# Second stage of a transformer kernel on one core: TensorE's waits ahead of runs of small matmuls, repeated waits dropped, every engine's work in another order

## The chip, the cores and the metric

The kernel runs on one core of a Trainium2 chip. The metric is the device time of the whole program in microseconds (us). The core has five engines with instruction streams of their own, which meet only at semaphores: TensorE (PE; its loads of stationary data are PEld), VectorE (DVE), ScalarE (ACT), GpSimd (POOL), and SyncE (SP), which here issues DMAs.

## The reference

The input has 8 samples of 512 tokens of 128 values, all in 32 bit. A first layer of attention (16 heads of 8, weights by an iteration on 1/(lambda - s)) comes first. Then come six layers of local attention and a gated feed-forward part; this is the second stage, and the change touches it alone:

```python
for i in range(6):
    x = attn_layer(shift_tokens(x), Wqkv[i], q_scale[i], k_scale[i], Wo[i]) + x
    x = ffn_layer(shift_tokens(x), ln_g[i], ln_b[i], W1[i], b1[i], W2[i], b2[i]) + x

def attn_layer(x, Wqkv, qs, ksc, Wo):      # 16 heads of 64
    q, k, v = split(x @ Wqkv)
    q, k = l2norm(q) * qs, l2norm(k) * ksc
    q, k = rotary(q), rotary(k)            # with a scale that grows with the position
    # windows of 32 tokens, each looks at itself and at the one before it
    attn = softmax(mask(8 * q @ k.T))
    return (attn @ v) @ Wo

def ffn_layer(x, g, bln, W1, b1, W2, b2):  # 341 hidden values
    a, gate = split(layernorm(x) * g + bln @ W1 + b1)
    return a * gelu(gate) @ W2 + b2
```

## The kernel before

Stage 1 does the first attention, stage 3 turns the result back and adds it. Stage 2 runs 48 steps: a step `n` is one sample through one layer (6 layers of 8 samples). The work of a step is cut in pieces, and each engine runs the pieces in an order that is written out in a function `body(b)` of its own. A body mixes pieces of step `b`, of `b - 1` and of `b - 2`, so that three steps are under way at once; `live(b, back)` leaves out those that do not exist. On TensorE and the other compute engines the first four bodies are peeled, and then a loop follows. TensorE's loop has a hint for its back edge, and its head stands at slot 0 of an instruction fetch block.

The pieces go by groups of four heads, `g` = 0 to 3:
- `q{g}`, `k{g}` (`project`, L1319): two matmuls of 512 columns each into two PSUM banks. ScalarE squares them (`squares`, L1550), k or q first by its order; VectorE multiplies them by two tables each (`rotate`, L1809 and L1810, which waits for the square); GpSimd adds the squares (`square_sums`, L1698) and the products (`add_rotated`, L1702).
- `norm{g}` (`norms`, L1326) sums the squares; ScalarE makes the inverse norm (L1555, L1564); VectorE finishes (`finish`, L1833), and eight DMAs (`rotated`, L1210) spread the result.
- `score{g}` (`scores`, L1342): 64 matmuls on tiles of 64 by 32, in two parts. VectorE masks and takes the maximum (L1817, L1824), GpSimd subtracts it (L1708), ScalarE takes the exponential (L1580), VectorE sums and inverts (L1839, L1846), GpSimd normalises (L1713).
- `turn{g}` (`turn`, L1354): eight transposes of 128 by 128; ScalarE copies them out (`turned`, L1586).
- `v{i}` (`values`, L1391); ScalarE copies it (L1573); DMAs roll it (`rolled`).
- `weigh{g}` (`weigh`, L1375): 64 matmuls of 32 columns, in two parts; VectorE copies them out (`weighted`, L1853).
- `wo` (L1401), `mean` (L1407), `var` (L1412), `gate0`, `gate1`, `up0`, `up1` (`hidden`, L1416) and `out` (`ffn_out`, L1441) are the output projection and the feed-forward part. VectorE's `residual` (L1864), `centre`, `scale`, `gate` (L1885) and `finished` (L1894), ScalarE's `log_variance`, `inverse_deviation` and `gelu`, and GpSimd's `affine` (L1723) go with them. At each new layer VectorE runs `tables(l)` ahead of its body.

A matmul of 32-bit data leaves two records of TensorE in the trace, and two of the load.

The eight PSUM banks are dealt by hand in a list, `HOLD`, in TensorE's order: the name of a piece, how many steps it lags, and its first bank. Pieces in `ONE` hold one bank, the others two. `take(name, b)` (the wait is L1306) looks back in the list for whoever held the banks last, and waits for the semaphore that says that they are empty (`EMPTIED`):

```python
EMPTIED |= {f"q{g}": [(s_rot[0], NG, g)], f"k{g}": [(s_rot[1], NG, g)],
            f"norm{g}": [(s_lnn, NG, g)], f"score{g}": [(s_mask, NG, g)], f"turn{g}": [(s_pTev, NG, g)],
            f"weigh{g}": [(s_oT, NG, g)], f"v{g}": [(s_vev, NG, g)]}
```

So the banks of a `q` are empty when VectorE has rotated it, and those of `up0` when VectorE has multiplied both gates. A wait on TensorE is an instruction of its own, `pe.wait_ge` followed by `pe.sem_inc(held["pe"], 1)`, and stands right ahead of the matmuls that need it.

Of the kernel before, what the change touches and what calls it, by code (L numbers as in the profile page):

```python
# [989 lines left out]
def stage2(nc, consts, wqkv, wod, w1d, w2d, vecd, hist):  # L990
    with ExitStack() as ctx:
# [116 lines left out]
        def live(b, back):  # L1108
# [31 lines left out]
        def _(sp):  # L1140
# [107 lines left out]
            def body(b, l, k):  # L1248
# [4 lines left out]
                if live(b, 3):  # L1253
                    store(b - 3)
                if live(b, 2):
                    load_w2(b - 2, l, k == 2)
                if live(b, 1):
                    rotated(b - 1, 2)
                if live(b, 0):
                    load_projections(b, l, k == 0, (2, 3))  # L1260
                if live(b, 0):
                    load_xs(b)
                if live(b, 1):
                    rolled(b - 1, 1)
                if live(b, 1):
                    rotated(b - 1, 3)
                if live(b, 0):
                    rotated(b, 0)
                if live(b, 0):
                    rotated(b, 1)  # L1270
                if live(b, 1):
                    load_vectors(b - 1, l, k == 1)
                if live(b, 0):
                    load_xr(b)
                if live(b, 0):
                    rolled(b, 0)
                if live(b, 1):
                    load_w1(b - 1, l, k == 1)
                if live(b, 0):
                    load_wo(b, l, k == 0)  # L1280
# [6 lines left out]
            for b in range(STEPS, STEPS + 3):  # L1287
                body(b, DEPTH, b - STEPS)
# [4 lines left out]
        def _(pe):  # L1293
# [16 lines left out]

            def project(n, g, which, out):
                pe.wait_ge(wg_in[g], 16 * n + 16)
                pe.sem_inc(held["pe"], 1)
                if g == 0:
                    pe.wait_ge(xs_in, 32 * n + 32)
                    pe.sem_inc(held["pe"], 1)
# [5 lines left out]
            def norms(n, g, out):  # L1322
                pe.wait_ge(s_sqs, at(n, g))
                pe.sem_inc(held["pe"], 1)
# [5 lines left out]
            def scores(n, g, part, out):  # L1330
                p = g % 2
                if part == 0:
                    pe.wait_ge(q_in[p], 128 * at(n, g // 2, 2))
                    pe.sem_inc(held["pe"], 1)
# [14 lines left out]
            def turn(n, g, out):  # L1349
                pe.wait_ge(s_pr, at(n, g))  # L1350
                pe.sem_inc(held["pe"], 1)
# [5 lines left out]
            def weigh(n, g, part, out):  # L1357
                if part == 0:
                    pe.wait_ge(s_pTev, at(n, g))
                    pe.sem_inc(held["pe"], 1)  # L1360
                if part == 0 and g % 2 == 0:
                    pe.wait_ge(s_vev, at(n, g + 1))
                    pe.sem_inc(held["pe"], 1)
                    pe.wait_ge(vr_in[g // 2], 48 * n + 96)
                    pe.sem_inc(held["pe"], 1)
# [16 lines left out]
            def values(n, i, out):  # L1382
                half, part = i // 2, i % 2
                if part == 0:
                    pe.wait_ge(wg_in[2 * half], 16 * n + 16)
                    pe.sem_inc(held["pe"], 1)
                    pe.wait_ge(wg_in[2 * half + 1], 16 * n + 16)
                    pe.sem_inc(held["pe"], 1)
# [55 lines left out]
            def body(b):  # L1444
# [24 lines left out]
                if live(b, 2):  # L1469
                    ups(b - 2, 1, take("up1", b))  # L1470
# [679 lines left out]
```

## Time and profile before

| | us |
|---|---|
| median of 3 runs | 4945.61 (4935.18 to 4952.09) |
| the profiled execution's own time | 4938.53 |
| its span, first to last instruction | 4936.4 |
| TensorE busy | 4103.4 (83%) |
| VectorE busy | 4056.8 (82%) |
| GpSimd busy | 3516.9 (71%) |
| ScalarE busy | 2979.7 (60%) |

Busy time of an engine is the time under its instructions; waits, branches and DMA issues do not count. Stage 2 takes up some two thirds of the span, from about 1540 to 4900 us. In the rows below, a bracket in a timeline is the engine's idle time ahead of that row, and what ended it; "issue" means that nothing the profile shows did.

### The profile page before, as it was taken

What the parts mean: (1) busy time and instruction counts of PE and PEld (TensorE: products, weight loads), DVE (VectorE), ACT (ScalarE), POOL (GpSimd) and SP (SyncE); (2) the same over time, 40 slices, a digit from 0 to 9 for tenths busy, and PEclk for the clock granted to TensorE, in tenths of its full rate; (3) what the DMA queues carried; (4) which work ended last, traced back from release to release, by engine and by line L of the source; (5) the groups of instructions that cost most, each with busy time, mean ns of one, the idle gap of its engine ahead of it and who ended that gap; (6) DMA issues with size and microseconds to landing.
All of it is one profiled execution on the core that took longest, in us unless ns stands there. A gap on an engine that the chain in (4) does not pass through costs nothing. (4 is left out here: it accounts for less than half of the span.)

```text
span 4936.4 us, 154683 instructions
## 1 busy us (share of the span) xinstructions
PE 4103.4 (83%) x60260; PEld 2147.1 (43%) x60260; DVE 4056.8 (82%) x7132; ACT 2979.7 (60%) x4240; POOL 3516.9 (71%) x1655
## 2 busy tenths in 40 slices
PE   3666666666647999899999999899998999899995
PEld 1233223233223555455544555455554555455552
DVE  6999999999956888788878888788887888788883
ACT  5999999999953555445544555455544555455441
POOL 4999999999965676666766676567665766576661
PEclk9755555555558999999999999999999999999997
DMA  0000000000004444444553444444444444444443
GB/s 14 3 5 9 5 9 5 5 9 5 7 8 107 114 113 109 113 103 109 116 123 92 107 113 109 99 114 111 109 114 97 113 109 109 98 118 109 108 98 82
DMA packets 234267, 382.36 MB, mean 77 GB/s; under 512 B 38432, under 2 KB 63776, under 8 KB 233504
## 3 DMA queue, kind: packets, MB, share of 16 engines
q1 hardware_dynamic: 229408, 371.06, 31.9%
q8 instruction: 488, 8.00, 0.7%
q10 hardware_dynamic: 4224, 2.10, 0.1%
q14 instruction: 147, 1.20, 0.1%
HBM read 51.89 MB, written 18.87 MB: 14 GB/s over the span
## 5 line engine op out<-in xcount | busy, mean ns | idle before, releaser
L734 POOL TENSOR_TENSOR W<-W 128x1280 f32<-128x1280 f32 x416 | 954.9, 2319 | 141.2 <-ACT W L585 139.9
L585 ACT ACTIVATE W<-S,lam 128x512 f32<-128x512 f32 (+3 forms) x2048 | 952.0, 553 | 84.2 <-DVE lam L878 72.9
L1702 POOL TENSOR_TENSOR m<-m 128x1024 f32<-128x1024 f32 x384 | 902.6, 2362 | 68.3 <-DVE m L1810 68.2
L849 DVE BATCH_NORM_STATS2 stats<-W 128x6 f32<-128x512 f32 (+3 forms) x2048 | 832.4, 478 | 57.6 <-POOL W L734 56.5
L1708 POOL TENSOR_TENSOR sm<-sm,mx 128x1024 f32<-128x1024 f32 x192 | 451.7, 2353 | 504.7 <-DVE mx L1824 504.7
L1319 PE MATMUL pb<-xs,wg 128*128 128x512 f32 x1536 | 760.4, 630 | 52.8 <-DMA xs<-hist 38.4
L1555 ACT ACTIVATE lnn<-pb,cst 128x1024 f32<-128x1024 f32 x192 | 213.9, 1114 | 806.7 <-PE pb L1326 806.7
L1833 DVE SCALAR_TENSOR_TENSOR nf<-rn,m 128x1024 f32<-128x1024 f32 x384 | 616.7, 1637 | 93.0 <-ACT rn L1564 77.7
L1550 ACT ACTIVATE sq<-pb 128x1024 f32<-128x1024 f32 x384 | 381.9, 1021 | 491.8 <-PE pb L1319 491.8
L1698 POOL TENSOR_TENSOR sqs<-sq 128x1024 f32<-128x1024 f32 x192 | 456.9, 2379 | 225.2 <-ACT sq L1550 225.2
L1713 POOL TENSOR_TENSOR pr<-pr,rsum 128x1024 f32<-128x1024 f32 x192 | 407.4, 2122 | 292.6 <-DVE rsum L1846 290.3
L1809 DVE TENSOR_TENSOR m<-pb,tab 128x1024 f32<-128x1024 f32 x384 | 464.7, 1210 | 16.9 <-ACT sq L1550 13.9
L1810 DVE TENSOR_TENSOR m<-pb,tab 128x1024 f32<-128x1024 f32 x384 | 465.6, 1212 | 0.0
L1319 PEld LDWEIGHTS pb<-xs,wg 128*128 128x128 f32 x1536 | 289.4, 199 | 360.3 <-issue 353.3
L1326 PE MATMUL pb<-sqs,ones 128*128 128x512 f32 x768 | 391.4, 633 | 29.7 <-DVE m L1810 22.8
L1853 DVE COPY oT<-pb 128x512 f32<-128x512 f32 x384 | 246.6, 683 | 176.5 <-PE pb L1375 176.5
L1391 PE MATMUL pb<-wg,xs 128*128 128x512 f32 x768 | 372.8, 608 | 19.4 <-issue 17.0
L1375 PE MATMUL pb<-pT,vr 64*64 64x32 f32 x12288 | 334.5, 220 | 58.9 <-issue 58.9
L374 PE MATMUL psD<-kT,qT 9*128 9x512 f32 (+3 forms) x1024 | 201.8, 747 | 191.0 <-DVE S L840 107.3
L1342 PEld LDWEIGHTS pb<-qkn 64*32 64x32 f32 x24576 | 260.3, 105 | 203.0 <-issue 202.2
L1401 PE MATMUL pb<-oT,wo 128*128 128x512 f32 x768 | 344.4, 602 | 1.5 <-DVE oT L1853 1.5
L1375 PEld LDWEIGHTS pb<-pT,v 64*64 64x64 f32 x12288 | 255.8, 135 | 191.8 <-issue 191.8
(120 smaller groups left out, 7124.4 us busy)
## 6 DMA issues: line engine op xcount, KB each, us to landing
qkn<-nf SPq DMA_DIRECT2D x1536, 128.0 KB, 2.4
vr<-v SPq DMA_DIRECT2D x96, 768.0 KB, 5.9
vr<-v SPq DMA_DIRECT2D x96, 192.0 KB, 5.5
xr<-hist SPq DMA_DIRECT2D x48, 256.0 KB, 2.9
hist<-xo SPq DMA_DIRECT2D x48, 256.0 KB, 3.8
wg<-wqkv SPq DMA_DIRECT2D x24, 384.0 KB, 3.8
xs<-hist SPq DMA_DIRECT2D x48, 128.0 KB
vr<-v SPq DMA_DIRECT2D x96, 64.0 KB, 6.2
```

Of the source, the lines that this page charges most:

```text
L585: ins = nc.scalar.activation(W[:, p, h, c], S[:, j % 2, h, c], ACT.Abs_reciprocal_sqrt, bias=lam[:, j, i:i + 1])
L734: nc.gpsimd.tensor_tensor(W[:, p, h, :], W[:, p, h, :], W[:, p, h, :], ALU.mult).then_inc(s_wp[p], 1)
L849: ins = nc.vector.bn_stats(out=stats[:, p, h * NBLK + u, :], in_=W[:, p, h, UOFF[u]:UOFF[u] + UNIT[u]])
L1319: mm = pe.matmul(out[:, half, :], wg[:, g, c:c + P], xs[:, 0:SEQ], start=True, stop=True)
L1375: mm = pe.matmul(out[64 * b:64 * b + 64, s, o:o + WIN], src[64 * s:64 * s + 64, k, c:c + DH2], pT[64 * s:64 * s + 64, b, r:r + WIN], start ...
L1698: nc.gpsimd.tensor_tensor(sqs[:, :, :], sq[:, :, 0, :], sq[:, :, 1, :], ALU.add).then_inc(s_sqs, 1)
L1702: nc.gpsimd.tensor_tensor(m1[:, which, :, :], m1[:, which, :, :], m2[:, which, ::-1, :], ALU.add)\
L1708: nc.gpsimd.tensor_tensor(x, x, mx[:, :].unsqueeze(2).broadcast_to([P, 16, 64]), ALU.subtract).then_inc(s_sub, 1)
L1713: nc.gpsimd.tensor_tensor(x, x, rsum[:, :].unsqueeze(2).broadcast_to([P, 16, 64]), ALU.mult).then_inc(s_pr, 1)
L1809: nc.vector.tensor_tensor(m1[:, which, :, :], src[:, :, :], tab[:, which, 0, :, :], ALU.mult)
L1810: nc.vector.tensor_tensor(m2[:, which, :, :], src[:, :, :], tab[:, which, 1, :, :], ALU.mult)\
L1833: nc.vector.scalar_tensor_tensor(out=nf[:, which, :, :], in0=rn[:, which, :].unsqueeze(1).broadcast_to([P, 2, SEQ]), scalar=1e12, in1=m1[: ...
```

## The change

It touches stage 2 only. All matmuls and all other computing instructions stay; what changes is where TensorE waits, which banks the pieces hold, and the order on every engine.

- The waits for data leave the functions of TensorE's pieces and become functions of their own (`weights_due`, `squares_due`, ...), called from `body`. Where a run of small matmuls (`weigh`, `score`, `turn`) stands ahead of a large piece, the large piece's `take` and its waits stand ahead of the small run, except that `turn0` to `var`, `turn1` to `v0`, the second part of `weigh2` to `norm1`, and `score0` to `turn3` keep theirs in between.
- Repeated waits (the same weights, inputs or `xn` for a second piece) go: by count 92 waits in a body become 77.
- `HOLD` has another order and other banks. `q3` and `k3` of a step move to the next body. `up1` comes before `k0`, `k0` before `q0`, `q1` moves behind `turn2`, and `out` no longer splits `score0`.
- The other engines' orders change too, among them: ScalarE squares k before q in groups 1 and 2; GpSimd normalises group 0 at the end of its body, behind both additions of group 2, and does `affine` ahead of `square_sums(3)`; VectorE rotates q before k in group 0, k before q in group 3, does `mask(b, 0)` ahead of `finished`, and `weighted(b, 0)` right after the rotations of group 3.
- SyncE issues the store one step earlier and in another place, `load_xs` right behind `rotated(b - 1, 2)`, and `rolled(b, 0)`, the store and `load_xr` at the end. `residual` on VectorE has one more wait. Three bodies are peeled in place of four.

```diff
         HOLD = [
-            ("var", 2, 3), ("turn0", 1, 0), ("v3", 1, 2), ("weigh0", 1, 4), ("norm3", 1, 0), ("gate1", 2, 7),
-            ("gate0", 2, 2), ("score2", 1, 4), ("q0", 0, 0), ("k0", 0, 4), ("up1", 2, 3), ("turn1", 1, 6),
-            ("v0", 0, 2), ("weigh1", 1, 6), ("norm0", 0, 4), ("k1", 0, 0), ("q1", 0, 4), ("score3", 1, 6),
-            ("v1", 0, 2), ("turn2", 1, 6), ("up0", 2, 2), ("weigh2", 1, 6), ("norm1", 0, 0), ("score0", 0, 2),
-            ("out", 2, 6), ("turn3", 1, 4), ("q2", 0, 0), ("weigh3", 1, 4), ("k2", 0, 6), ("wo", 1, 3),
-            ("score1", 0, 0), ("norm2", 0, 6), ("mean", 1, 3), ("q3", 0, 4), ("v2", 0, 2), ("k3", 0, 6),
+            ("turn0", 1, 2), ("var", 2, 0), ("q3", 1, 6), ("k3", 1, 0), ("weigh0", 1, 2), ("v3", 1, 4),
+            ("norm3", 1, 0), ("gate0", 2, 6), ("gate1", 2, 3), ("score2", 1, 0), ("up1", 2, 2), ("k0", 0, 4),
+            ("q0", 0, 0), ("turn1", 1, 6), ("v0", 0, 2), ("weigh1", 1, 6), ("k1", 0, 0), ("norm0", 0, 4),
+            ("score3", 1, 2), ("v1", 0, 6), ("turn2", 1, 2), ("q1", 0, 4), ("weigh2", 1, 2), ("up0", 2, 6),
+            ("norm1", 0, 6), ("out", 2, 0), ("score0", 0, 4), ("turn3", 1, 2), ("q2", 0, 6), ("weigh3", 1, 2),
+            ("k2", 0, 0), ("wo", 1, 5), ("score1", 0, 6), ("norm2", 0, 0), ("mean", 1, 3), ("v2", 0, 4),
         ]
...
+            def due(s, value):
+                pe.wait_ge(s, value)
+                pe.sem_inc(held["pe"], 1)
+
+            def weights_due(n, g):
+                due(wg_in[g], 16 * n + 16)
+
+            def inputs_due(n):
+                due(xs_in, 32 * n + 32)
+
+            def squares_due(n, g):
+                due(s_sqs, at(n, g))
...
             def norms(n, g, out):
-                pe.wait_ge(s_sqs, at(n, g))
-                pe.sem_inc(held["pe"], 1)
                 for which in range(2):
                     mm = pe.matmul(out[:, which, :], ones4[:, :], sqs[:, which, :], start=True, stop=True)
...
             def body(b):
...
-                if live(b, 1):
-                    turn(b - 1, 1, take("turn1", b))
-                if live(b, 0):
-                    values(b, 0, take("v0", b))
-                if live(b, 1):
-                    weigh(b - 1, 1, 0, take("weigh1", b))
...
+                if live(b, 1):
+                    take("turn1", b)
+                    probabilities_due(b - 1, 1)
+                    turn(b - 1, 1, bank("turn1"))
+                if live(b, 0):
+                    take("v0", b)
+                    weights_due(b, 1)
+                    values(b, 0, bank("v0"))
+                if live(b, 0):
+                    take("k1", b)
+                if live(b, 1):
+                    take("weigh1", b)
+                    turned_due(b - 1, 1)
+                    weigh(b - 1, 1, 0, bank("weigh1"))
+                if live(b, 0):
+                    project(b, 1, 1, bank("k1"))
...
+                if live(b, 2):
+                    take("up0", b)
+                if live(b, 1):
+                    take("weigh2", b)
+                    turned_due(b - 1, 2)
+                    values_due(b - 1, 1)
+                    weigh(b - 1, 2, 0, bank("weigh2"))
+                if live(b, 2):
+                    ups(b - 2, 0, bank("up0"))
                 if live(b, 1):
                     weigh(b - 1, 2, 1, bank("weigh2"))
                 if live(b, 0):
-                    norms(b, 1, take("norm1", b))
-                if live(b, 0):
-                    scores(b, 0, 0, take("score0", b))
+                    take("norm1", b)
+                    squares_due(b, 1)
+                    norms(b, 1, bank("norm1"))
                 if live(b, 2):
-                    ffn_out(b - 2, take("out", b))
+                    take("out", b)
+                    gated_due(b - 2)
+                    ffn_out(b - 2, bank("out"))
...
             def residual(n):
+                dve.wait_ge(s_xo, at(n - 1, 0, 1))
+                dve.sem_inc(held["dve"], 1)
                 dve.wait_ge(xr_in, n * 16 + 16)
...
                 if live(b, 0):
+                    rotate(b, 0, 0)
+                if live(b, 0):
                     rotate(b, 0, 1)
-                if live(b, 0):
-                    rotate(b, 0, 0)
```

## Rows read from the trace of the kernel before

**Rows 1.** The page: busy us, share, count; instruction queue: packets, MB, share.

```profile
PE 4103.4 (83%) x60260; PEld 2147.1 (43%) x60260; DVE 4056.8 (82%) x7132; ACT 2979.7 (60%) x4240; POOL 3516.9 (71%) x1655
...
q8 instruction: 488, 8.00, 0.7%
```

**Rows 2.** Busy time in a stretch of stage 2: length, engines, clock, DMA.

```profile
2000.00:4900.00 2900.00, 2703.25 (x47340) 1466.28 (x47338) 2352.91 (x2453) 1418.94 (x1471) 1902.60 (x855) 0.97 0.45 106
```

**Rows 3.** Line L1407: duration ns min/median/max, first and last start.

```profile
L1407 PE MATMUL pb<-xm,avg x96: 592/592/667, 1603.8 to 4875.1; 128*128 128x512 f32 x96
```

**Rows 4.** TensorE's timeline, one step from score2 to score2: start, us, what.

```profile
3000.26 1.48 PE L1342 MATMUL pb<-qkn 64*32 64x64 f32 x128
3002.06 3.67 PE L1319 MATMUL pb<-xs,wg 128*128 128x512 f32 x8 [0.31 <-issue]
...
3006.42 1.04 PE L1354 MATMUL pb<-ident,pr 128*128 128x128 f32 x8
3007.82 1.95 PE L1391 MATMUL pb<-wg,xs 128*128 128x512 f32 x4 [0.36 <-issue]
3009.71 0.43 PE L1375 MATMUL pb<-pT,v 64*64 64x32 f32 x16
...
3020.73 1.06 PE L1354 MATMUL pb<-ident,pr 128*128 128x128 f32 x8
3022.28 1.95 PE L1416 MATMUL pb<-xn,w 128*128 128x512 f32 x4 [0.48 <-ACT v L1573]
...
3028.07 0.86 PE L1342 MATMUL pb<-qkn 64*32 64x64 f32 x64
3029.34 2.81 PE L1441 MATMUL pb<-gl,w 128*128 128x512 f32 x6 [0.41 <-issue]
...
3032.92 1.06 PE L1354 MATMUL pb<-ident,pr 128*128 128x128 f32 x8
3033.82 1.88 PE L1319 MATMUL pb<-xs,wg 128*128 128x512 f32 x4
...
3067.63 1.48 PE L1342 MATMUL pb<-qkn 64*32 64x64 f32 x128
```

**Rows 5.** TensorE's timeline, the end of weigh3 and k2 of that step.

```profile
3037.29 0.28 PE L1375 MATMUL pb<-pT,vr 64*64 64x32 f32 x5
3038.82 0.42 PE L1375 MATMUL pb<-pT,vr 64*64 64x32 f32 x11 [1.25 <-issue]
3039.28 1.96 PE L1319 MATMUL pb<-xs,wg 128*128 128x512 f32 x4
```

**Rows 6.** The same place in another step.

```profile
3395.72 0.41 PE L1375 MATMUL pb<-pT,vr 64*64 64x32 f32 x16
3396.12 1.95 PE L1319 MATMUL pb<-xs,wg 128*128 128x512 f32 x4
```

**Rows 7.** Waits, whole span: us in total, times, longest.

```profile
PE pb L1375 <- issue: 62.3, 44, 2.6
```

**Rows 8.** TensorE's timeline, k2 of a third step.

```profile
3259.62 3.42 PE L1319 MATMUL pb<-xs,wg 128*128 128x512 f32 x4
```

**Rows 9.** Busy time and granted clock around it, columns as in rows 2.

```profile
3259.00:3263.00 4.00, 3.80 (x16) 1.78 (x16) 3.38 (x4) 0.00 (x0) 0.89 (x1) 0.62 0.95 204
```

**Rows 10.** ScalarE's timeline: both squares of group 0.

```profile
3005.76 1.94 ACT L1550 ACTIVATE sq<-pb 128x1024 f32<-128x1024 f32 x2 [1.23 <-PE pb L1319]
```

**Rows 11.** VectorE's timeline: a product of the rotation, and two gates.

```profile
2598.02 1.22 DVE L1810 TENSOR_TENSOR m<-pb,tab 128x1024 f32<-128x1024 f32 x1
...
3024.27 1.41 DVE L1885 SCALAR_TENSOR_TENSOR gl<-pb,vec,gl 128x512 f32<-128x512 f32 x2 [0.32 <-PE pb L1416]
```

**Rows 12.** TensorE's timeline, norm0 of a step that begins a layer.

```profile
2599.53 3.75 PE L1326 MATMUL pb<-sqs,ones 128*128 128x512 f32 x4 [4.99 <-DVE m L1810]
```

**Rows 13.** The page's groups: count, busy us, mean ns, idle before.

```profile
L1702 POOL TENSOR_TENSOR m<-m 128x1024 f32<-128x1024 f32 x384 | 902.6, 2362 | 68.3 <-DVE m L1810 68.2
```

More of the change, by code:

```diff
@@ L1286, in _ @@
                     body(l * BATCH + k, l, k)
-            for b in range(STEPS, STEPS + 3):
+            for b in range(STEPS, STEPS + 2):
                 body(b, DEPTH, b - STEPS)
@@ L1444, in body @@
             def body(b):
+                if live(b, 1):
+                    take("turn0", b)
+                    probabilities_due(b - 1, 0)
+                    turn(b - 1, 0, bank("turn0"))
                 if live(b, 2):
[L1446 removed]
+                    take("var", b)
+                    deviation_due(b - 2)
+                    variance(b - 2, bank("var"))
                 if live(b, 1):
[L1448 removed]
+                    take("q3", b)
+                    project(b - 1, 3, 0, bank("q3"))
                 if live(b, 1):
[L1450 removed]
+                    take("k3", b)
+                    project(b - 1, 3, 1, bank("k3"))
                 if live(b, 1):
[L1452 removed]
+                    take("v3", b)
+                if live(b, 1):
+                    take("weigh0", b)
+                    turned_due(b - 1, 0)
+                    values_due(b - 1, 0)
+                    weigh(b - 1, 0, 0, bank("weigh0"))
                 if live(b, 1):
@@ L1455, in body @@
                 if live(b, 1):
-                    norms(b - 1, 3, take("norm3", b))
+                    values(b - 1, 3, bank("v3"))
+                if live(b, 1):
+                    take("norm3", b)
+                    squares_due(b - 1, 3)
+                    norms(b - 1, 3, bank("norm3"))
                 if live(b, 2):
-                    gates(b - 2, 1, take("gate1", b))
+                    take("gate0", b)
+                    normed_due(b - 2)
+                    gates(b - 2, 0, bank("gate0"))
@@ L1459, in body @@
                 if live(b, 2):
-                    gates(b - 2, 0, take("gate0", b))
+                    take("gate1", b)
+                    gates(b - 2, 1, bank("gate1"))
+                if live(b, 2):
+                    take("up1", b)
                 if live(b, 1):
-                    scores(b - 1, 2, 0, take("score2", b))
+                    take("score2", b)
+                    rotated_due(b - 1, 2)
+                    scores(b - 1, 2, 0, bank("score2"))
                 if live(b, 1):
@@ L1477, in body @@
                 if live(b, 0):
-                    norms(b, 0, take("norm0", b))
+                    project(b, 1, 1, bank("k1"))
+                if live(b, 0):
+                    take("norm0", b)
+                    squares_due(b, 0)
                 if live(b, 1):
@@ L1507, in body @@
                 if live(b, 1):
-                    turn(b - 1, 3, take("turn3", b))
+                    take("turn3", b)
+                    probabilities_due(b - 1, 3)
+                    turn(b - 1, 3, bank("turn3"))
                 if live(b, 0):
-                    project(b, 2, 0, take("q2", b))
+                    project(b, 2, 0, bank("q2"))
+                if live(b, 0):
+                    take("k2", b)
                 if live(b, 1):
-                    weigh(b - 1, 3, 0, take("weigh3", b))
+                    take("weigh3", b)
+                    turned_due(b - 1, 3)
+                    weigh(b - 1, 3, 0, bank("weigh3"))
                 if live(b, 1):
@@ L1682, in _ @@
             act.wait_ge(cleared, 1)
-            for b in range(4):
+            for b in range(3):
                 body(b)
-            with act.Fori(4, STEPS) as b:
+            with act.Fori(3, STEPS) as b:
                 body(b)
@@ L1782, in _ @@
             pool.wait_ge(cleared, 1)
-            for b in range(4):
+            for b in range(3):
                 body(b)
-            with pool.Fori(4, STEPS) as b:
+            with pool.Fori(3, STEPS) as b:
                 body(b)
@@ L1988, in _ @@
             tables(0)
-            for b in range(4):
+            for b in range(3):
                 body(b)
-            with dve.Fori(4, BATCH) as b:
+            with dve.Fori(3, BATCH) as b:
                 body(b)
```

240 lines of the change are left out of this document (119 added, 121 removed).

## The prediction

> **What bounds the kernel now.** I read the page first. TensorE and VectorE are both busy for over four fifths of the span [rows 1], but that is an average over three stages, and the change touches only the second. So the next view is the busy time of a stretch inside stage 2: over 2900 us TensorE (PE) is busy 2703, VectorE (DVE) 2353, GpSimd (POOL) 1903, ScalarE (ACT) 1419, at 0.97 of the full clock [rows 2]. Stage 2 is bound by TensorE, with VectorE close behind.
>
> The length of a step (one sample through one layer) comes from the averaging matmul L1407, which runs once a step: from 1603.8 to 4875.1 are 47 steps of 69.6 us, layer changes included [rows 3]. A step without a layer change is read from the two starts of `score2`, 3000.26 and 3067.63: 67.37 us [rows 4]. The reader is to see in that timeline what TensorE's idle brackets stand behind: each follows a run of small matmuls (`score`, `turn`), has 0.31 to 0.48 us, and sits ahead of an operation that carries three to five waits. Behind a matmul of 512 columns the waits are invisible, since the queue of issued matmuls covers them; behind small ones nothing does. `turn1` to `v0` with four waits takes 1.40 us, `turn3` to `q2` with two takes 0.90 [rows 4].
>
> One gap is of another kind. In the second half of `weigh3` TensorE stops for 1.25 us in the middle of a run of small matmuls, where the code has no wait [rows 5]; in another step the same run goes through in one piece [rows 6]. The view of waits has 44 such stalls, 1.42 us each [rows 7], so nearly every step has one. Counted in the source (a load and a matmul record for each pass, and one instruction for each wait) the loop's body has some 2,400 instructions, and the eighth multiple of 256 behind its head, which the code puts at slot 0 of a fetch block, falls within the last thirty instructions of `weigh3`. The instruction queue moved 8.00 MB in 488 packets, 16 KB each, which is 256 instructions of 64 bytes [rows 1]. I read the gap as a block of instructions that comes late: 67.37 - 1.53 (3037.29 to 3038.82) = 65.84 us is the step without it. Behind some of these stalls `k2` takes 3.42 us for its four matmul records and not 1.96 [rows 5, 8]: the granted clock, 0.62 over those 4 us [rows 9], went down to the lower of its two levels, 1.2 GHz, for a part of them, and that costs another 1.5 to 1.7 us.
>
> **The change, part by part.** The trace speaks of all of stage 2 alike, so I price one step and multiply by 47. The sum is made against the profiled execution's own 4938.5 us, which is 7 us under the median of the runs.
>
> *Waits taken out or put under cover.* The brackets ahead of `q0`, `v0`, `up0` and the output projection `out` are 0.31, 0.36, 0.48 and 0.41 us [rows 4], 1.56 in all. The modelled end of a run lies up to 0.16 us behind the next start where nothing is in between (`turn3` ends at 3033.98 by its row, `q2` starts at 3033.82), so the true cost is up to 0.6 more, and a few single waits add some 0.2. In the new order `up1`, `q1`, `q2`, `v1`, `k1` and `norm2` follow their small run without any wait, `out` follows `norm1`, and of all transitions from small to large only `turn1` to `v0` (three) and `weigh2` to `norm1` (three) keep more than two. The gain is 1.56 to 2.4 us a step; I take 2.35, since the code removes all four. Fifteen wait instructions fewer are worth nothing of their own: they sat behind large matmuls. TensorE's matmuls stay as they are; small runs are as many as before (13), so no gain or loss from their number. A step of TensorE with no stall is then 65.84 - 2.35 = 63.5 us.
>
> *Banks that come free too late.* The waits for banks now stand ahead of the small run, and the banks were dealt anew, so I followed every bank from its holder to its next taker. Three distances are now shorter than the chain of work that frees the bank. Its links: a large matmul's end to ScalarE's start 0.03 us (3005.73 to 3005.76), one square 0.97 to 1.02 [rows 4, 10]; one product of the rotation 1.22, the next starting some 1.13 behind; VectorE's end to TensorE's matmul 0.29 (2599.24 to 2599.53) [rows 11, 12]; each further wait about 0.15 (the two transitions above: 0.50 us for two waits, less what one of them waited for data).
> - `k1` takes the banks of `q0`, and its wait now stands ahead of `weigh1`, with two more behind it. From the end of `q0`: 0.03 + 1.02 + 2.35 + 0.29 + 0.3 = 4.0 us. TensorE has `turn1` (0.90) and `v0` (1.89, 3007.82 to 3009.71) in between [rows 4], 2.8 at most. Stall 0.9 to 1.3; I take 1.1. Before, 9 us of work stood there. VectorE also turned its order to `q0` first although `k0` is now made first, so it starts late for both.
> - `gate0` takes the banks of `q3`, which VectorE rotates after `k3`. From the end of `k3`: 0.03 + 1.02 + four products 4.6 + 0.29 + 0.3 = 6.2. In between are `weigh0` (2.0), `v3` (1.9) and `norm3` (1.7), 5.5 with overlaps. Stall 0.6 to 0.9; I take 0.8. Waiting for the square sums of group 3, now behind the affine step on GpSimd, falls into the same gap.
> - `norm1` takes the banks of `up0`. VectorE's two gate products start 0.04 behind the end of `up0` and take 1.41 [rows 4, 11], then 0.29 and 0.3 for further waits: 2.05 us against half of `weigh2`, 1.0. Stall 1.0.
>
> Two more are near: `turn0` needs group 0's probabilities, now last in GpSimd's order behind both additions of group 2, and ScalarE squares `k2` ahead of `q2` (from `k2`'s end 2 x 1.0 + 4.6 + three GpSimd operations of up to 2.36 [rows 13] = 13.8 us against some 12.8 of TensorE work); `k2` needs the banks of `out` ahead of `weigh3`, while VectorE does the mask first. Each costs nothing to 1.0 us; I take 0.5 for both, as the GpSimd operation that normalises is often shorter. All stalls: 2.5 to 4.4, taken 3.4.
>
> *The moved DMA issues and the rest.* The sync queue's order changes around stores, loads of `xr`, the two `w` loads and `rolled`. `load_xs` now stands behind `rotated(2)` alone, but `k0` comes 1 us nearer to `v3`; I see 1.5 us of slack and take nothing. A late `xs` shows in the view of waits only where a layer begins. At a layer change, VectorE's tables stand ahead of the rotations: TensorE stops for 4.99 us at `norm0` [rows 12]. It will stop instead at `weigh1`, for the same tables; nothing, with 3 us either way over five changes. The new wait in `residual` is for something a step old. One peeled step fewer is nothing at run time.
>
> *The block boundary.* By the same count the eighth boundary falls again within the last thirty instructions of `weigh3`, so I keep the 1.42 us and the clock drops. The Trainium skill, Runtime: NRT & Kernel Launch, section Instruction fetch mechanics, says that the sequencer fetches the next 16 KiB block while it executes the current one, and that the issue floor hides this. By that rule there would be no such stall in either kernel; the trace, with 44 of 1.42 us [rows 7], does not agree for runs of small matmuls.
>
> *Sum:* -2.35 + 3.4 = +1.05 us a step, times 47 = +49: 4938.5 + 49 = 4987, and I say 4986.
>
> **The rivals.**
> 1. *The chains are not late* (ScalarE and VectorE turn out free earlier, or the stalls overlap): the change does what its waits promise, -2.35 us a step, 4828. Against it: the three chains start at a matmul and run through single, measured links, with no slack to find. Chance 0.13.
> 2. *The late block goes away* because the order ahead of it gives the fetch more time: -1.42 and about 0.6 of clock drops a step (I choose a third of 1.7) on top of my sum: -1.0 a step, 4892. For it: a few steps go without the stall now [rows 6], so it is near an edge. Chance 0.20. This ends on the other side of mine; it decides once the fetch comes 1.4 us sooner.
> 3. *Stalls of 1 us in all*, below my bound of 2.5 since the links overlap, and a draw with the gain: within 15 us of 4938. Chance 0.12.
> 4. *A second late block.* `score0` is no longer split by `out`; its 256 instructions run in 1.5 us, and they fill one fetch block almost exactly. If the next one comes late, 0.6 to 2 us a step on top: about 5045. The new gaps may also bring more clock drops. Chance 0.12.
>
> **How the numbers follow.** Forecast 0.43, rivals as above. Likeliest alone: 4960 to 5030. What a measurement of this kernel can tell from no change is about 0.3%, 15 us. Slower by more: 0.43 + 0.12 = 0.55; within: 0.12; faster: 0.33. The range for 8 in 10 leaves out rival 1 for the most part and the far end of rival 4: 4865 to 5060.
>
> **What would show it.** Right: TensorE idle ahead of `weigh1`, `gate0` (or `norm3`) and `norm1`, released by VectorE's products and gates, 0.6 to 1.2 us in every step; no bracket ahead of `q0`/`k0`, `up0` and `out`; L1407's counterpart at a distance of 70.6 us; still some 44 stalls within a run of small matmuls. Wrong: no waits of TensorE on VectorE (rival 1), no gap in `weigh3` (rival 2), or a gap at the end of `score0` (rival 4).

## The result: 7.3% slower, and the profile after

The changed kernel takes 5305.24 us (median; 5300.08 to 5306.21), the one before 4946.43 beside it. The ratio is 1.0726 (95%: 1.0706 to 1.0746), 359 us. The sign was forecast, the size was not: +41 us, and the measured time lies above the range.

Line numbers have moved: `project` is L1361, `norms` L1366, `scores` L1379, `turn` L1389, `weigh` L1402, `values` L1413, the output projection L1419, `mean` L1423, `hidden` L1430, `ffn_out` L1442; VectorE's `rotate` is L1884 and L1885, its mask L1892, `gate` L1962. The page of the kernel after, engines and instruction queue (compare [rows 1]):

```profile
PE 4206.3 (79%) x60260; PEld 2192.1 (41%) x60260; DVE 3919.4 (74%) x7132; ACT 2979.9 (56%) x4240; POOL 3468.4 (65%) x1655
...
q8 instruction: 489, 8.01, 0.7%
```

The averaging matmul as in [rows 3], after:

```profile
L1423 PE MATMUL pb<-xm,avg x96: 592/592/1061, 1609.0 to 5245.1; 128*128 128x512 f32 x96
```

47 steps in 3636.1 us are 77.4 us a step, against 69.6: 7.8 more, times 47 = 365 us. The whole loss is in the steps. These 47 steps as stretches, before and then after, columns as in [rows 2]:

```profile
1603.80:4875.10 3271.30, 3068.49 (x54128) 1669.29 (x54127) 2686.31 (x2792) 1622.85 (x1679) 2175.76 (x977) 0.98 0.46 108
```

```profile
1609.00:5245.10 3636.10, 3167.21 (x54129) 1711.77 (x54127) 2549.54 (x2793) 1623.12 (x1679) 2129.00 (x978) 0.95 0.41 97
```

No engine has more work. TensorE's idle time in them, length less busy time, grows from 202.8 to 468.9 us, which is 5.7 us a step. Its busy time for the same matmuls grows by 98.7 us, 2.1 a step, at a granted clock of 0.95 and not 0.98. The two make up the 7.8. One step of the kernel after on TensorE's timeline, from `mean` to the next `mean`, 77.2 us:

```profile
3467.75 1.02 PE L1423 MATMUL pb<-xm,avg 128*128 128x512 f32 x2
...
3479.41 1.95 PE L1366 MATMUL pb<-sqs,ones 128*128 128x512 f32 x4
3481.91 2.81 PE L1430 MATMUL pb<-xn,w 128*128 128x512 f32 x6 [0.55 <-DVE m L1885]
3484.65 1.49 PE L1379 MATMUL pb<-qkn 64*32 64x64 f32 x128
3486.07 1.09 PE L1430 MATMUL pb<-xn,w 128*85 128x512 f32 x2
...
3490.43 1.04 PE L1389 MATMUL pb<-ident,pr 128*128 128x128 f32 x8
3491.30 1.88 PE L1413 MATMUL pb<-wg,xs 128*128 128x512 f32 x4
3494.49 0.43 PE L1402 MATMUL pb<-pT,v 64*64 64x32 f32 x16 [1.31 <-DVE m L1885]
...
3511.36 1.96 PE L1366 MATMUL pb<-sqs,ones 128*128 128x512 f32 x4 [0.84 <-DVE gl L1962]
...
3515.82 1.47 PE L1379 MATMUL pb<-qkn 64*32 64x64 f32 x127
3518.87 0.21 PE L1379 MATMUL pb<-qkn 64*32 64x64 f32 x1 [1.58 <-issue]
...
3522.36 0.43 PE L1402 MATMUL pb<-pT,v 64*64 64x32 f32 x16 [0.43 <-issue]
...
3526.07 0.66 PE L1402 MATMUL pb<-pT,vr 64*64 64x32 f32 x16 [1.87 <-issue]
3526.66 3.78 PE L1361 MATMUL pb<-xs,wg 128*128 128x512 f32 x4
...
3541.26 0.66 PE L1379 MATMUL pb<-qkn 64*32 64x64 f32 x40 [2.02 <-issue]
3541.85 3.32 PE L1366 MATMUL pb<-sqs,ones 128*128 128x512 f32 x4
3544.96 1.00 PE L1423 MATMUL pb<-xm,avg 128*128 128x512 f32 x1
```

The reader is to see three things. First, large pieces follow small runs without a bracket: L1430 behind `score2`, L1413 behind `turn1`. That is what the change does. Second, the three forecast waits for VectorE: 0.55 ahead of `gate0`, 1.31 ahead of `weigh1`, 0.84 ahead of `norm1`. Third, three stops within runs of small matmuls where the code has no wait: 1.58 in the last matmul of `score0`, 1.87 in `weigh3`, 2.02 in `score1`. Before there was one, of 1.42 [rows 7]. Behind two of them a large piece runs at about half speed: `k2` takes 3.78 us, `norm2` 3.32.

The view of waits of the kernel after, over the whole span (us, times, longest):

```profile
PE pb L1379 <- issue: 186.8, 127, 4.8
...
PE pb L1402 <- issue: 93.6, 87, 2.2
PE pb L1402 <- DVE m L1885: 89.3, 47, 7.2
...
PE pb L1366 <- DVE gl L1962: 41.4, 46, 0.9
...
PE pb L1430 <- DVE m L1885: 25.9, 46, 0.7
...
PE pb L1389 <- issue: 17.5, 16, 2.2
```

Counted in the trace from the loop's head, the three stops lie at instructions 1792 to 1816, 2048 to 2072 and 2304 to 2328: 0 to 24 behind a multiple of 256. The few of `turn` (L1389) lie right behind the loop's head. For the first stop of the step above, the view of DMA from 3515 to 3520 (40 slices of 0.125 us) shows the only packet of that time, one of the instruction queue:

```profile
GB/s 0 0 0 0 0 0 0 0 0 0 0 131 0 0 0 0 0 0 0 0 0 0 0 0 0 0 0 0 0 0 0 0 0 0 0 0 0 0 0 0
...
q8 instruction: 1, 0.02, 1.3%
```

It starts in the slice at 3516.4, and TensorE goes on at 3518.87, 2.5 us later. By the same records of the 135 such stops in `score0`, `weigh3` and `score1`, TensorE goes on 2.3 to 2.85 us (nine in ten; all of them 2.2 to 3.1, median 2.5) behind the start of the last packet of that queue; in the kernel before it is 2.3 to 2.7 (nine in ten, median 2.4). And TensorE runs 256 small instructions in some 1.4 us.

### The profile page after: what moved, and what is told of

Its sections match the earlier page's. It is cut to its first block and busy times, and to the rows that moved or that the text cites. A ratio compares the mean times of both kernels' runs of the same rounds, so it can differ in the third digit from the quotient of the medians.

```text
span 5302.9 us, 154074 instructions
## 1 busy us (share of the span) xinstructions
PE 4206.3 (79%) x60260; PEld 2192.1 (41%) x60260; DVE 3919.4 (74%) x7132; ACT 2979.9 (56%) x4240; POOL 3468.4 (65%) x1655
## 5 line engine op out<-in xcount | busy, mean ns | idle before, releaser
L1783 POOL TENSOR_TENSOR sm<-sm,mx 128x1024 f32<-128x1024 f32 x192 | 408.8, 2129 | 786.7 <-DVE mx L1899 786.7
L1361 PE MATMUL pb<-xs,wg 128*128 128x512 f32 x1536 | 783.3, 646 | 17.6 <-DMA xs<-hist 15.8
L1625 ACT ACTIVATE sq<-pb 128x1024 f32<-128x1024 f32 x384 | 388.1, 1024 | 705.7 <-PE pb L1361 705.2
L1884 DVE TENSOR_TENSOR m<-pb,tab 128x1024 f32<-128x1024 f32 x384 | 467.8, 1218 | 236.1 <-ACT sq L1625 233.4
L1908 DVE SCALAR_TENSOR_TENSOR nf<-rn,m 128x1024 f32<-128x1024 f32 x384 | 472.5, 1261 | 115.0 <-ACT rn L1639 109.8
L1892 DVE TENSOR_TENSOR sm<-pb,wmask 128x1024 f32<-128x1024 f32 x192 | 234.9, 1224 | 386.1 <-PE pb L1379 386.1
L1379 PE MATMUL pb<-qkn 64*32 64x64 f32 x24576 | 316.7, 229 | 206.7 <-issue 186.8
L1885 DVE TENSOR_TENSOR m<-pb,tab 128x1024 f32<-128x1024 f32 x384 | 466.0, 1213 | 0.0
L1366 PE MATMUL pb<-sqs,ones 128*128 128x512 f32 x768 | 425.3, 681 | 47.3 <-DVE gl L1962 41.4
L1361 PEld LDWEIGHTS pb<-xs,wg 128*128 128x128 f32 x1536 | 296.1, 204 | 324.6 <-issue 320.1
L1402 PE MATMUL pb<-pT,v 64*64 64x32 f32 x12288 | 336.1, 222 | 111.3 <-DVE m L1885 89.3
L1402 PEld LDWEIGHTS pb<-pT,v 64*64 64x64 f32 x12288 | 267.7, 136 | 335.7 <-issue 335.7
L1402 PE MATMUL pb<-pT,vr 64*64 64x32 f32 x12288 | 337.6, 222 | 76.3 <-issue 76.3
L1379 PEld LDWEIGHTS pb<-qkn 64*32 64x32 f32 x24576 | 268.3, 107 | 294.3 <-issue 294.2
```

The lines of the kernel that those rows point to most:

```text
L1361: mm = pe.matmul(out[:, half, :], wg[:, g, c:c + P], xs[:, 0:SEQ], start=True, stop=True)
L1366: mm = pe.matmul(out[:, which, :], ones4[:, :], sqs[:, which, :], start=True, stop=True)
L1379: mm = pe.matmul(out[o:o + 32, b, (2 * k + s) * 64:(2 * k + s + 1) * 64], qkn[64 * b:64 * b + 64, p, hh, 0, (w + 1) * WIN:(w + 2) * WIN], ...
L1402: mm = pe.matmul(out[64 * b:64 * b + 64, s, o:o + WIN], src[64 * s:64 * s + 64, k, c:c + DH2], pT[64 * s:64 * s + 64, b, r:r + WIN], start ...
L1884: nc.vector.tensor_tensor(m1[:, which, :, :], src[:, :, :], tab[:, which, 0, :, :], ALU.mult)
L1885: nc.vector.tensor_tensor(m2[:, which, :, :], src[:, :, :], tab[:, which, 1, :, :], ALU.mult)\
```

## The experiments

The theory after the result: late instruction blocks carry most of the loss, the three waits for VectorE most of the rest. Its rival: the waits for data carry it all.

**1. Half a block further.** One number of the changed kernel; every boundary moves by 128 instructions.

```diff
-                         head_slot={mybir.EngineType.PE: 0}) as b:
+                         head_slot={mybir.EngineType.PE: 128}) as b:
```

> The changed kernel with one number altered: the head of TensorE's loop stands at instruction 128 of a fetch block, not at 0, so that every block boundary moves by half a block. Work, orders, banks and waits are the same. Theory (late blocks): the stalls of the changed kernel at instructions 1792, 2048 and 2304 behind the head, some 6.6 us a step, come from blocks that hold only small matmuls or that are asked for behind a wait. Half a block away, each block holds a large piece too, most of the stalls go, and with them some of the clock drops: 4.4 to 8 us a step less, 4930 to 5100 us. Rival (the three data chains carry the 359 us): nothing changes, 5305. Second rival (late blocks only move to other small runs): three stalls a step at instructions 1664, 1920 and 2176, 5250 to 5320.

Measured: 5068.62 us, ratio to the kernel before 1.0257 (1.0213 to 1.0302). Steps of 72.4 us, 4.9 less than the changed kernel. Its waits:

```profile
PE pb L1379 <- issue: 116.3, 91, 5.1
...
PE pb L1402 <- DVE m L1885: 89.3, 47, 6.9
```

All three stops are gone from their places, and a new one of some 2.1 us stands in `score3`, at instruction 1160, in most steps; the largest wait for VectorE is what it was. The 47 steps as a stretch:

```profile
1610.70:5014.60 3403.90, 3070.38 (x54128) 1674.51 (x54127) 2539.82 (x2793) 1629.91 (x1679) 2137.76 (x978) 0.98 0.44 103
```

TensorE's busy time is back at that of the kernel before, 3070.4 against 3068.5 us. So 237 of the 359 us hang on where the blocks begin, with no instruction moved: idle time and the lower clock both.

**2. The same number in the kernel before.**

> The kernel before with the head of TensorE's loop at instruction 128 of a fetch block in place of 0; nothing else. Theory (late blocks): the one stall a step in weigh3, 1.42 us, goes, and part of the clock drops with it: 1.4 to 2.1 us a step less, 4845 to 4880 us. Rival (any boundary costs the same wherever it lies): 4946. Second rival (the new boundaries fall worse): slower, 4960 to 5050.

Measured: 4865.1 us, ratio 0.9858 (0.9817 to 0.9900). The stops of `weigh3` [rows 7] fall from 62.3 us to

```profile
PE pb L1375 <- issue: 15.0, 12, 2.0
```

The granted clock between 2000 and 4800 us goes from 0.98 to 0.99. This is the fastest kernel of the study, and it beats both. Against it the changed kernel with its head at 128 too (experiment 1) is 204 us slower, where at head 0 it is 359: what the change costs depends on the position, and at neither does it gain.

**3. A third position, chosen to be bad.** The kernel before with its head at slot 170.

> The kernel before with the head of TensorE's loop at instruction 170 of a fetch block; nothing else. By the trace score2 lies at instructions 345 to 601 of the loop and score1 at 2132 to 2388; with this head two blocks (342 to 598 and 2134 to 2390) hold these runs and next to nothing else, while the other boundaries lie much as they do with the head at 128 relative to large pieces. Theory (a block holding one run of 256 small instructions is crossed in 1.4 us, while the next one needs some 3.5 us from the crossing to being usable: 1.1 us to its fetch and 2.4 us from there): two stalls of 1.5 to 2.3 us a step, at the ends of score2 and score1, and more clock drops, so 3.0 to 6.5 us a step above the head at 128 (4865): 5005 to 5170 us. Rival (a block is late in weigh3 for a reason of its own, data or DMA traffic at that time, and position in the block does not matter): 4865 to 4950 us, with no stall at either place.

Measured: 5056.6 us, ratio 1.0251 (1.0217 to 1.0286), inside the theory's range and 191 us above experiment 2 with the same instructions in the same order. Timeline of one step:

```profile
3623.49 1.10 PE L1412 MATMUL pb<-xc,avg 128*128 128x512 f32 x2 [2.26 <-issue]
...
3633.83 1.55 PE L1342 MATMUL pb<-qkn 64*32 64x64 f32 x128
...
3639.12 4.33 PE L1319 MATMUL pb<-xs,wg 128*128 128x512 f32 x6 [2.29 <-issue]
```

One of the two stops is where it was forecast, behind `score2` (2.29). The other is not behind `score1` but later, at `var`, the first piece behind the loop's branch (2.26): I take the late block there for that of the loop's head.

**4. Two waits moved back.** The changed kernel, head at 0.

```diff
                 if live(b, 0):
-                    take("norm2", b)
-                    squares_due(b, 2)
-                if live(b, 0):
                     take("score1", b)
...
                 if live(b, 0):
+                    take("norm2", b)
+                    squares_due(b, 2)
                     norms(b, 2, bank("norm2"))
```

> The changed kernel with the two waits for norm2 (its bank and its square sums) moved from ahead of score1 to behind it. Theory (a blocked sequencer asks for no block): the request for the block at instruction 2304 no longer stands behind the wait for VectorE, and the stall of 2.2 us in the second half of score1 goes or shrinks to under 1 us, with some of the clock drops: 1.5 to 3.5 us a step less, 5140 to 5230 us, although norm2 now pays for its waits in the open (up to 0.5 us). Rival (the block is late because the matmuls ahead are short, not because of the wait): the stall stays, 5290 to 5330.

Measured: 5249.74 us, ratio 1.0629 (1.0580 to 1.0678); 55 us less, where 75 to 165 were expected. Its waits:

```profile
PE pb L1389 <- issue: 104.2, 46, 4.4
...
PE pb L1379 <- issue: 79.0, 54, 4.7
```

The stop in `score1` is gone (L1379 falls by 108 us), but the next block, that of the loop's head, is now the late one, 46 times of 2.3 us ahead of `turn0` (L1389). A stop that goes can hand its block's lateness to the next.

**5. One wait out of a held place.** With the head at 128 the remaining stop waits for a block whose packet starts 3.4 to 3.7 us behind the crossing, and not 1.1. I took the waits ahead of `score3` for the cause, the one for `v1`'s bank above all, and moved that one.

```diff
-                if live(b, 0):
-                    take("v1", b)
                 if live(b, 1):
                     take("score3", b)
...
-                    values(b, 1, bank("v1"))
+                    values(b, 1, take("v1", b))
```

> The changed kernel with its loop head at instruction 128 and one wait moved: the wait for v1's bank stands right ahead of v1 and no longer ahead of score3. With the head at 128 one stall of 2.3 us a step is left, in the second half of score3; the block it waits for is fetched 1.2 us after TensorE's sequencer has passed the three waits ahead of score3, and the last to come true of them is the one for v1's bank, which VectorE empties late (weighted of group 1); norm0 hides that wait from TensorE. Theory (a block is asked for about 1.1 us behind the crossing, but not while the sequencer stands at a wait): the wait gone, the block is asked for some 2 us earlier and the stall of 2.3 us goes; v1 pays 0 to 0.3 us for its wait in the open: 1.5 to 2.8 us a step less than with the head at 128 alone, 4935 to 5000 us. Rival (the block is late because score3's 256 instructions run in 1.3 us, wherever the waits stand): 5060 to 5085 us.

Measured: 5068.73 us, ratio 1.0289 (1.0265 to 1.0313): the rival. The stop stays (L1379 108.5 us in 91 waits, 116.3 before). This theory fell here: it was not that wait.

**6. Something large in the short block.** The changed kernel, head at 128, `v1` between the halves of `score3`.

> The changed kernel with its loop head at instruction 128 and v1 between the two halves of score3, not behind it; waits where they are. At that head the block from 896 to 1152 is asked for 3.7 us behind the crossing, 1.0 us into score3, and the second half of score3 stops for 2.3 us. Theory (the time is short because nothing large lies between the request and the end of the block): v1's 1.9 us lie there now, and the stall shrinks to 0 to 0.6 us: 1.5 to 2.5 us a step less than with the head at 128 alone (5069), 4950 to 5000 us. Rival (v1 in between holds the request back in its turn, as wo and norm0 seem to): the stall stays at 2 us or more, 5050 to 5090 us.

Measured: 5069.93 us, ratio 1.0271 (1.0245 to 1.0297). By the time the rival; the trace says otherwise:

```profile
3457.53 0.86 PE L1379 MATMUL pb<-qkn 64*32 64x64 f32 x64
3458.32 1.99 PE L1413 MATMUL pb<-wg,xs 128*128 128x512 f32 x4
3460.23 0.63 PE L1379 MATMUL pb<-qkn 64*32 64x64 f32 x36
3461.16 0.45 PE L1379 MATMUL pb<-qkn 64*32 64x64 f32 x28 [0.30 <-issue]
3463.22 1.77 PE L1389 MATMUL pb<-ident,pr 128*128 128x128 f32 x8 [1.62 <-DVE sm L1892]
```

The stop shrank from some 2.1 to 0.30, as the theory said, and `turn2` now waits 1.62 us for VectorE's mask of `score3`, 48 times in the span (77.2 us). I read it so: the stop had hidden this wait, and with it gone the chain through VectorE is the limit.

**7. `out` back between the halves of `score0`.** The changed kernel, head at 0; one part of the change undone.

```diff
-("norm1", 0, 6), ("out", 2, 0), ("score0", 0, 4),
+("norm1", 0, 6), ("score0", 0, 4), ("out", 2, 0),
...
+                if live(b, 0):
+                    take("q2", b)
+                    weights_due(b, 2)
                 if live(b, 2):
                     take("out", b)
                     gated_due(b - 2)
-                    ffn_out(b - 2, bank("out"))
```

> The changed kernel, loop head at instruction 0 as it is, with one part of the change undone: out stands again between the two halves of score0 (in TensorE's order and in the list of banks), its waits ahead of the first half. The block from instruction 1536 to 1792 then holds out's matmuls within it. Theory (it is late because score0's 256 instructions fill it and run in 1.3 us): the stall of 1.7 us a step at instruction 1792 goes or shrinks below 0.5, with part of the clock drops: 1.2 to 2.5 us a step less than the changed kernel (5305), 5190 to 5250 us. Rival (the request for that block is held back by the waits and large pieces ahead, and comes as late as now): the stall stays, 5290 to 5320 us.

Measured: 5326.18 us, ratio 1.0776 (1.0734 to 1.0818), 21 us above the changed kernel. Timeline:

```profile
3541.62 1.96 PE L1366 MATMUL pb<-sqs,ones 128*128 128x512 f32 x4 [0.94 <-DVE gl L1963]
3546.19 0.85 PE L1379 MATMUL pb<-qkn 64*32 64x64 f32 x64 [2.61 <-issue]
3546.97 2.85 PE L1442 MATMUL pb<-gl,w 128*128 128x512 f32 x6
```

ScalarE's timeline at that place:

```profile
3543.62 1.11 ACT L1631 ACTIVATE lnn<-pb,cst 128x1024 f32<-128x1024 f32 x1 [0.51 <-PE pb L1366]
```

The stop within `score0` is gone, as the theory said, but TensorE idles 2.61 us ahead of it. The waits of `q2`, `out` and `score0` now stand in a row behind `norm1`, and the first is for the banks of `norm1` itself, which `q2` takes over (`("norm1", 0, 6)`, `("q2", 0, 6)`): ScalarE has read them at 3544.73, and TensorE goes on 1.46 us later. In between its stream has nine wait records and one register instruction, about 0.15 us each. In the changed kernel `out` stands between `norm1` and that wait and covers it. The theory left this wait out.

**8. The chain through `q0`.** The changed kernel, head at 128, `q0` made ahead of `k0` (and squared first), as VectorE takes them.

```diff
                 if live(b, 0):
-                    take("k0", b)
+                    take("q0", b)
                     weights_due(b, 0)
                     inputs_due(b)
+                    project(b, 0, 0, bank("q0"))
+                if live(b, 0):
+                    take("k0", b)
                     project(b, 0, 1, bank("k0"))
-                if live(b, 0):
-                    take("q0", b)
-                    project(b, 0, 0, bank("q0"))
...
```

> The changed kernel with its loop head at instruction 128, and q0 made ahead of k0 again (TensorE's pieces, the list of banks, ScalarE's squares of group 0); VectorE rotates q0 first as it does in the changed kernel. Theory (the chain q0 end, square, product, then k1's bank): the chain starts 1.7 us earlier, the wait of 1.3 us ahead of weigh1 goes to under 0.3, and a step is 1.0 to 1.4 us shorter than with the head at 128 alone, 5000 to 5025 us. Rival (VectorE is held up by something else, so that the product of q0 ends as late as now): 5060 to 5080 us.

Measured: 5015.82 us, ratio 1.0165 (1.0133 to 1.0196); 53 us less than experiment 1, as forecast. Its waits:

```profile
PE pb L1361 <- DVE sm L1892: 47.0, 47, 1.7
...
PE pb L1402 <- DVE m L1885: 28.7, 5, 5.7
```

Of 47 waits ahead of `weigh1` the five of the layer changes are left; 1.0 us a step for the mask has come up ahead of a projection.

**9. The first part of the change alone**, in the old orders and banks: all waits ahead of the small runs, repeated ones dropped. Head at 0, and at 128.

```diff
+                if live(b, 0):
+                    take("norm0", b)
+                    squares_due(b, 0)
+                if live(b, 1):
+                    take("weigh1", b)
+                    turned_due(b - 1, 1)
                 if live(b, 1):
-                    weigh(b - 1, 1, 0, take("weigh1", b))
+                    weigh(b - 1, 1, 0, bank("weigh1"))
                 if live(b, 0):
-                    norms(b, 0, take("norm0", b))
+                    norms(b, 0, bank("norm0"))
```

> The kernel before, its orders and banks on every engine as they were, with the first part of the change alone: TensorE's waits ahead of the runs of small matmuls and the repeated waits dropped; head of the loop at instruction 0 as in both kernels. Theory: of the brackets of 0.31, 0.36, 0.48 and 0.41 us ahead of large pieces most go (a gain of 1.5 to 2.3 us a step), but waits dropped and moved shift what lies at the block boundaries and hold back their requests, so that late blocks can take 0 to 4 us a step: 4830 to 5050 us. Rival (late blocks do not come with the waits but with the new order): the gain alone, 4835 to 4875 us. Second rival (waits moved ahead of small runs block what they should cover): TensorE's waits on other engines grow, above 5050 us.

> The kernel before with all of TensorE's waits moved ahead of the small runs and the repeated ones dropped, loop head at instruction 128. With its head at 0 this kernel took 5040 us, 72.1 us a step, of which 1.2 us a step are late blocks in weigh3. Theory: those go with part of the clock drops, the waits for VectorE and GpSimd (some 2.7 us a step) stay: 1.2 to 2.0 us a step less, 4945 to 4985 us. Rival (the new boundaries fall on runs that are held back by the moved waits): 5040 us or more.

Measured: 5040.35 us, ratio 1.0189 (1.0137 to 1.0240), and 5128.07 us, ratio 1.0397 (1.0370 to 1.0424). The first is within its range, a wide one; the second misses its range, and its rival (5040 us or more) came true. Waits of the first:

```profile
PE pb L1400 <- DVE m L1909: 77.1, 51, 6.5
...
PE pb L1400 <- POOL sqs L1797: 46.7, 42, 2.4
```

Moving waits costs by itself: 77.1 against 22.8 us before for VectorE's products, 46.7 for GpSimd's square sums (before, the view lists no such wait ahead of `weigh`). At 128, where the old code had nearly no late block, this one has two places, in `score3` and `weigh2`, 2.0 us a step by my count of the trace: with the waits moved and dropped, a good position has become a bad one.

**10. Only waits that come true early**, in the old order, head at 128; then with the wait for `xs` back in its place and the head at 136.

```diff
                 if live(b, 0):
                     take("q0", b)
                     weights_due(b, 0)
-                    inputs_due(b)
...
                 if live(b, 0):
+                    inputs_due(b)
                     project(b, 0, 0, bank("q0"))
```

> The kernel before with its loop head at instruction 128, the repeated waits dropped, and of the moved waits all but three: norm3's, norm0's with k1's, and norm1's stand again right ahead of their pieces, since with all waits moved TensorE stood for VectorE and GpSimd there (1.1 us ahead of weigh1, 1.0 ahead of weigh2, 0.7 ahead of weigh0). Theory: what is left are waits that come true early, which take 0.3 to 0.5 us each out of score2 to q0, turn2 to up0 and score0 to out, less what more than three waits behind a large piece cost: about 1.0 us a step less than the kernel before with its head at 128 (4865), 4800 to 4835 us. Rival (hoisting waits gains nothing by itself, since the queue takes as long for them elsewhere): 4855 to 4880 us. Second rival (boundaries fall badly after the shift by some 15 instructions): 4890 to 4950 us.

> The kernel before with the repeated waits dropped and TensorE's waits moved ahead of small runs only where they come true early. It differs from the kernel that moved some waits (4972 us) in two points: the wait for the inputs xs stands again right ahead of q0, because TensorE stood 2.3 us a step for it ahead of score2, and the loop head is at instruction 136, so that the boundaries lie about where they lay in the kernel before with its head at 128. Theory: 1.8 to 2.2 us a step come back from xs, and 0 to 1.2 us from late blocks in score3 and weigh2: 4820 to 4885 us. Rival (moved waits gain nothing, late blocks stay): 4885 to 4900 us.

Measured: 4972.41 us, ratio 1.0087 (1.0066 to 1.0109), a miss by 137 us, and 4877.99 us, ratio 0.9876 (0.9841 to 0.9910). In the first, TensorE waits for a load whose wait had been moved across `score2`:

```profile
PE pb L1377 <- DMA xs<-hist: 97.5, 44, 6.4
```

With that undone most comes back, but nothing is gained over experiment 2 (4865.1): by my count of the trace 1.1 us a step of late blocks in `score3` and `weigh2` are there, against 0.3 in experiment 2.

## Why the prediction was wrong, step by step

**What bounds the kernel** was right: TensorE, with VectorE close behind. That VectorE comes up within 1.0 to 1.6 us a step once TensorE is relieved (6, 8) was not said.

**Waits taken out, -2.35 us a step.** The brackets ahead of `v0`, `up0`, `q0` or `k0` and `out` are gone. In the view of waits of the kernel before they are

```profile
PE pb L1416 <- ACT v L1573: 23.6, 46, 0.6
...
PE pb L1441 <- issue: 19.4, 46, 0.5
...
PE pb L1391 <- issue: 17.0, 46, 0.5
...
PE pb L1319 <- issue: 12.8, 39, 0.4
```

together 72.8 us, 1.5 a step, and not 2.35; what the sum added for modelled ends does not show in this view. Five waits for `xs` at layer changes, 0.4 us a step, went too, which the sum had at nothing. The sentence that waits are invisible behind a matmul of 512 columns holds only for waits that have come true by then. One that comes true late is seen, and each wait behind it adds 0.15 us: 0.43 us ahead of `weigh3`, which waits for VectorE to empty the bank of `out` (in experiment 1 the bracket at the same place reads `[0.54 <-DVE xo L1971]`), and 2.61 us behind `norm1` (7). And no kernel in which waits were moved ahead of small runs, and nothing else, came out faster than its twin (9, 10).

**Banks that come free too late, +3.4.** Right in place and nearly in size. Forecast 1.1, 0.8, 1.0 and 0.5 for the rest; in the step shown 1.31, 0.55, 0.84 and 0.43, 3.1 in all. Over the span it is (89.3 - 22.8 + 41.4 + 25.9) / 47 = 2.8 us a step for the three, 22.8 being what stood there before, at the layer changes [rows 12], and 0.4 for the last. Experiment 8 takes one of the links away, and its 1.3 us go.

**The block boundary, +0.** This is the step that failed: "I keep the 1.42 us and the clock drops". I located the eighth boundary, found it in the same piece, and stopped; the seventh and ninth had to be priced as well, and the time between the request for a block and its need. Counted in the trace, the 135 stops within the three runs are 237 us and those of `turn0` behind the loop's head 17.5: 5.4 us a step, against 62.3 / 47 = 1.3 before. That is +4.1. (The rest of what the view puts down to "issue" stands ahead of small runs, `weigh3` and `score1`, and is no late block.) The clock adds 2.1 us a step of busy time. That this part goes with the stops is shown by experiment 1: the same matmuls in the same order, and all of it goes.

The sum with the measured terms: 4.1 + 2.1 + 2.8 + 0.4, and 0.3 ahead of `score1`, less 1.5 and 0.4, is 7.8, as measured. By this sum, without the 6.2 of the block boundary the change would have cost some 1.6 us a step, where the sum had 1.05. So the sign of the forecast came from terms that were about right, and the size failed at the boundary.

**Rival 4** (a second late block, chance 0.12) named the place in `score0` and the cause; 1.58 us there is within its 0.6 to 2. But there were three late blocks, not two, and the clock cost 2.1 us a step; the rival gave 5045. Rivals 1 to 3 did not come: chains and blocks were both there. The Trainium skill, Runtime: NRT & Kernel Launch, section Instruction fetch mechanics, has the next block fetched while the current one runs, hidden by the issue floor; experiments 2 and 3 disagree with this by 191 us for the same instructions.

**What stays open.** What holds a block's request back. By my count in the changed kernel, only behind the crossings at 256, 768, 1024 and 1280 does the next packet start within 1.1 to 1.7 us. For the three late blocks, at 1792, 2048 and 2304, it starts 3.4, 6.5 and 13.6 us behind the crossing one block earlier. So they are late also because they are asked for late, not only because small instructions run through a block quickly. Between 2048 and the last of these packets stand the end of `weigh3`, `k2` and the output projection with its waits. Taking two waits away (4) brought it 3 us forward; taking one away elsewhere (5) did nothing. Whether it is the waits, the long matmuls, the late block before, or several of these was not settled, and so the late blocks of 9 and 10 can't be forecast from the source.

## What to carry to other kernels

In a loop with runs of hundreds of small instructions, price every block boundary, not the one that hurts now; any edit that changes an order or a count of instructions deals them anew. Try the position of the loop's head first, since it costs nothing: here it was worth 1.4% in one kernel and 4.5% in the other, and no reordering or moved wait of experiments 4 to 8 gained more than about 1%. A wait moved ahead of a cover must come true before the cover begins; else it trades 0.4 us of bracket for a stop of 1 to 2 us. And a stop that disappears may only have hidden the next chain.

## What the hardware showed that I had not expected

- 16 KB of instructions are usable 2.3 to 2.85 us behind the start of their packet at most stops within a run (some 3.3 at the loop's head in experiment 3, by my count), while TensorE runs 256 small instructions in 1.4 us.
- The same code at three head positions took 4865, 4946 and 5057 us.
- A late block costs more than its stop: the two large pieces behind such stops ran 3.78 and 3.32 us in place of some 1.96, at a granted clock of 0.66 over the 7 us around the first:

```profile
3523.00:3530.00 7.00, 5.13 (x103) 3.12 (x96) 3.57 (x5) 0.00 (x0) 0.72 (x1) 0.66 0.61 132
```
